# New instruction orders on five queues of an adaLN block with six local-attention layers, and one row transfer started before a wait

## The reference, cut to what matters

```python
h = layernorm(x) * (1 + ca) + sa;  x = x + ga * attention(h)      # 8 batches of 512 rows, 128 wide
h = layernorm(x) * (1 + cb) + sb                                  # goes through six layers of:
    h = attn_layer(shift_tokens(h), Wqkv[i], q_scale[i], k_scale[i], Wo[i]) + h
    h = ffn_layer(shift_tokens(h), ln_g[i], ln_b[i], W1[i], b1[i], W2[i], b2[i]) + h
x = x + gb * h
...
def attn_layer(x, Wqkv, qs, ksc, Wo):      # 16 heads of 64, windows of 32 rows
    q, k, v = split(x @ Wqkv)              # 128 -> 3 * 1024
    q = l2norm(q) * qs;  k = l2norm(k) * ksc
    q, k = rotate(q), rotate(k)            # cos part + rotated-half sin part
    p = softmax(8 * q @ k.T, masked)       # each window sees itself and the window before
    return (p @ v) @ Wo                    # 1024 -> 128
def ffn_layer(x, g, b, W1, b1, W2, b2):
    a, gate = split(layernorm(x) * g + b) @ W1 + b1)   # 128 -> 2 * 341
    return a * gelu(gate) @ W2 + b2
```

## Time and profile before

| | |
|---|---|
| time, median of 3 runs | 3615.62 us (3609.76 to 3617.31) |
| profiled execution: its own time / its span | 3607.98 us / 3606.2 us |
| PE busy | 3238.4 us (90% of the span) |
| DVE busy | 3119.3 us (86%) |
| POOL busy | 2468.9 us (68%) |
| ACT busy | 2391.9 us (66%) |
| granted PE clock, mean | 0.98 of full |
| DMA engines busy | 16 to 19% in the layers |

### The profile page before, as it was taken

How to read it: one execution, slowest core, us unless ns; L and a number is a source line. 1 busy time by engine, 2 the same in 40 slices (tenths; PEclk the granted TensorE clock), 3 DMA queues, 4 the chain that set the end, 5 groups by cost and what they waited for, 6 DMA issues and landing times.

```text
span 3606.2 us, 108351 instructions
## 1 busy us (share of the span) xinstructions
PE 3238.4 (90%) x46108; PEld 2099.0 (58%) x46108; DVE 3119.3 (86%) x2914; ACT 2391.9 (66%) x3945; POOL 2468.9 (68%) x1265
## 2 busy tenths in 40 slices
PE   5658999999999999999989999999999999999986
PEld 3325566666656666656656655666665666665663
DVE  6759989989989989989988998998998998998992
ACT  4645666666666766666666766666666666666664
POOL 4456776777777777767776777777776777776771
PEclk9879999999999999999999999999999999999997
DMA  2001111122111112111121111111211121111111
GB/s 76 1 1 36 39 37 40 37 55 53 38 37 39 41 48 55 40 39 37 36 54 49 42 39 38 40 49 48 48 37 37 38 53 49 44 39 40 37 38 40
DMA packets 150433, 148.32 MB, mean 41 GB/s; under 512 B 39228, under 2 KB 95424, under 8 KB 149952
## 3 DMA queue, kind: packets, MB, share of 16 engines
q1 hardware_dynamic: 149952, 141.39, 15.9%
HBM read 19.62 MB, written 2.10 MB: 6 GB/s over the span
## 4 chain that ended last, share of the span: by engine, by line
PE 48%; DVE 17%; issue 11%; SPq 9%; ACT 4%; DMA 3%; POOL 1%; ACTq 0%; DVEq 0%; POOLq 0%
PE bank L574 15%; PE mid L624 8%; PE bank L673 5%; PE mid L583 5%; PE bank L644 5%; SPq L345 4%; PE mid L611 4%; DMA PT<-PTd 3%; DVE PTd L1384 3%; DVE rot L1411 3%; PE bank L681 3%; DVE rot L1405 3%; PE mid L631 2%; SPq L352 2%; SPq L348 2%
## 5 line engine op out<-in xcount | busy, mean ns | idle before, releaser
L1155 POOL TENSOR_TENSOR swp<-raw,TS 128x1024 f32<-128x1024 f32 x384 | 899.8, 2368 | 823.7 <-DVE raw L1397 823.7
L574 PE MATMUL bank<-wqkv,xs 128*128 128x512 f32 x2304 | 1172.3, 614 | 82.0 <-ACT V L917 63.6
L1145 POOL TENSOR_TENSOR rr<-ssm,nhalf 128x32 f32<-128x32 f32 x192 | 1051.8, 5478 | 16.0
L903 ACT ACTIVATE raw<-bank 128x512 f32<-128x512 f32 x768 | 454.0, 598 | 341.0 <-PE bank L574 273.2
L574 PEld LDWEIGHTS bank<-wqkv,xs 128*128 128x128 f32 x2304 | 380.8, 190 | 366.1 <-issue 206.4
L1391 DVE TENSOR_REDUCE ss<-sq 128x16 f32<-128x1024 f32 x384 | 466.1, 1214 | 47.6 <-ACT sq L911 46.8
L583 PEld LDWEIGHTS mid<-ident,rot 128*128 128x128 f32 x3072 | 354.0, 141 | 225.9 <-issue 163.8
L1411 DVE TENSOR_TENSOR rot<-rot,swp 128x2048 f32<-128x2048 f32 x192 | 440.1, 2292 | 21.1 <-DVE rot L1405 1.4
L1397 DVE TENSOR_TENSOR raw<-raw,rr 128x2048 f32<-128x2048 f32 x192 | 438.0, 2281 | 14.4 <-POOL rr L1145 14.4
L624 PEld LDWEIGHTS mid<-PT,V 128*64 128x64 f32 x6144 | 338.4, 138 | 190.5 <-issue 139.3
L624 PE MATMUL mid<-PT,V 128*64 128x128 f32 x6144 | 382.4, 277 | 69.2 <-DMA PT<-PTd 61.8
(11 more groups left out here) (134 smaller groups left out, 4251.7 us busy)
## 6 DMA issues: line engine op xcount, KB each, us to landing
PT<-PTd SPq DMA_DIRECT2D x1344, 64.0 KB
xs<-F SPq DMA_DIRECT2D x192, 64.0 KB, 1.9
wqkv<-d_wqkv SPq DMA_DIRECT2D x36, 256.0 KB, 3.2
VT<-V SPq DMA_DIRECT2D x144, 64.0 KB
BT<-PTd SPq DMA_DIRECT2D x288, 32.0 KB
fwo<-d_fwo SPq DMA_DIRECT2D x6, 512.0 KB, 5.0
d_out<-X SPq DMA_DIRECT2D x8, 256.0 KB, 2.3
w<-d_w SPq DMA_DIRECT2D x6, 341.0 KB
```

What stands on the lines that cost most here:

```text
L574: nc.tensor.matmul(bank[bk][:, :], xs[:, j, :], wqkv[:, c, :], start=True, stop=True)\
L903: nc.scalar.activation(raw[:, j % 2, c * 512:(c + 1) * 512], bank[RAW_BANK[c]][:, :], ACT.Copy)\
L1145: pool.tensor_tensor(rr[:, :], ssm[:, :], nhalf[:, :], ALU.pow).then_inc(rr_ready, 1)
L1155: last = pool.tensor_tensor(dst[:, :, :, t, :], src[:, :, :, 1 - t, :], tab.unsqueeze(2).broadcast_to([P, 2, HEADS, 32]), ALU.mult)
```

## The change

Nothing is added to or taken from the computation; the number of instructions of each kind is the same. The change permutes the calls inside each `slot(c)`, moves some FFN stages into the next slot, and permutes a few DMAs. The PSUM bank of each projection follows from the new order.

```diff
-        LAST_QK = 1
+        LAST_QK = 2
         LAST_VO = 1
-        LAST_V = 4
-        RAW_BANK = (1, 0, 0, 1, 1, 0)
+        LAST_V = 5
+        RAW_BANK = (1, 0, 1, 0, 0, 1)
...
             def bands(n, j):
 
-                sp.wait_ge(pT_ready, n + 1)
                 wait(sp, pv_done, n)
                 if j > 0:
                     sp.wait_ge(v_out[1], n)
                     sp.dma_start(VT[P - 2 * W:P - W, :], V[P - W:P, 1 - j % 2, 512:1024]).then_inc(band_moved, 16)
+                sp.wait_ge(pT_ready, n + 1)
...
                 fetch(l, 4)
+                move(l, 0)
                 next_fwo(l)
-                move(l, 0)
```

More of the change, by code:

```diff
@@ L713, in slot @@
                     step(c, 4, out_proj)
+                    after_batch(c, (2, xn_ready), (3, yo_ready), (3, lin_out[2]), (3, ge_ready[2]), (3, ge_ready[1]), (3, ge_ready[0]), (3, lin_out[0]), (3, lin_out[1]), (3, nT_out))
+                    batch(c, 2, norm_back_ffn)
                 elif c % TPB == 1:
-                    after(c, (4, v_out[1]), (1, raw_out[2]), (1, raw_out[1]))
+                    after(c, (4, v_out[0]), (1, raw_out[3]), (1, raw_out[1]))
                     step(c, 0, proj, 1, True, 0)
+                    after_batch(c, (2, nT_out), (2, xn_ready), (3, yo_ready), (3, lin_out[2]), (3, ge_ready[2]), (3, ge_ready[1]), (3, ge_ready[0]), (3, lin_out[0]), (3, lin_out[1]))
@@ L717, in slot @@
+                    batch(c, 2, ffn_in, 1, 0, True, 7)
+                    after(c, (4, v_out[1]), (1, raw_out[2]), (1, raw_out[0]))
+                    step(c, 0, proj, 0, False, 1)
+                    after_batch(c, (2, lin_out[1]), (2, nT_out), (2, xn_ready), (3, yo_ready), (3, lin_out[2]), (3, ge_ready[2]), (3, ge_ready[1]), (3, ge_ready[0]), (3, lin_out[0]))
+                    batch(c, 2, ffn_in, 0, 0, False, 7)
                     after(c, (4, prob_ready))
                     step(c, 3, scores)
-                    after(c, (4, v_out[0]), (1, raw_out[3]), (1, raw_out[0]))
@@ L720, in slot @@
[L720 to L724, removed]
@@ L733, in slot @@
-                    after_batch(c, (2, lin_out[1]), (2, nT_out), (2, xn_ready), (3, yo_ready), (3, lin_out[2]), (3, ge_ready[2]), (3, ge_ready[1]), (3, ge_ready[0]), (3, lin_out[0]))
-                    batch(c, 2, ffn_in, 0, 0, False, 7)
+                    after(c, (3, qkT_out[1]), (5, oT_out), (3, qkT_out[3]))
+                    step(c, 2, qk_back, 3, True)
+                    after(c, (3, qkT_out[2]), (5, oT_out), (3, qkT_out[0]))
+                    step(c, 2, qk_back, 0, False)
+                    after(c, (0, raw_out[1]), (4, v_out[0]), (1, raw_out[3]))
@@ L735, in slot @@
+                    step(c, 0, proj, 3, False, 0)
+                    after(c, (0, raw_out[0]), (4, v_out[1]), (1, raw_out[2]))
+                    step(c, 0, proj, 2, False, 1)
                     after(c, (2, qkT_out[0]), (3, qkT_out[2]), (5, oT_out))
@@ L1006, in slot @@
                     step(c, 0, to_raw, 0, False)
+                    batch(c, 2, attn_to_sbuf)
                     step(c, 0, squares, 0)
+                    step(c, 2, qk_to_sbuf, 3)
                     step(c, 2, qk_to_sbuf, 0)
[L1009 removed]
+                    step(c, 0, to_raw, 3, False)
+                    step(c, 3, exps)
                     step(c, 0, to_raw, 2, False)
[L1011 to L1012 removed]
+                    step(c, 0, squares, 1)
                     step(c, 4, o_to_sbuf)
[L1014 removed]
                     step(c, 3, to_v, 4)
[L1016 removed]
+                    batch(c, 2, ffn_normed)
+                    batch(c, 2, ffn_affine)
                     step(c, 3, to_v, 5)
                     step(c, 2, qk_to_sbuf, 1)
[L1019 to L1020 removed]
+                    step(c, 2, qk_to_sbuf, 2)
+                    batch(c, 2, lin_to_sbuf, 1)
                 elif c % TPB == 1:
@@ L1060, in slot @@
                     step(c, 0, to_raw, 0, False)
+                    batch(c, 2, ffn_to_sbuf)
                     step(c, 0, squares, 0)
+                    step(c, 2, qk_to_sbuf, 3)
                     step(c, 2, qk_to_sbuf, 0)
-                    step(c, 2, qk_to_sbuf, 3)
+                    step(c, 0, to_raw, 3, False)
+                    step(c, 3, exps)
                     step(c, 0, to_raw, 2, False)
-                    step(c, 3, exps)
-                    step(c, 0, to_raw, 3, False)
+                    step(c, 0, squares, 1)
                     step(c, 4, o_to_sbuf)
-                    step(c, 0, squares, 1)
                     step(c, 3, to_v, 4)
-                    step(c, 2, qk_to_sbuf, 2)
                     step(c, 3, to_v, 5)
                     step(c, 2, qk_to_sbuf, 1)
-                    batch(c, 1, attn_to_sbuf)
+                    step(c, 2, qk_to_sbuf, 2)
             act.wait_ge(zero_ready, 1)
```

166 lines of the change are left out of this document (75 added, 91 removed).

## The result

The changed kernel takes 3455.81 us, the median of 4 runs (3452.98 to 3457.16), beside 3613.09 us for the kernel before on the same chip (4 runs, 3609.76 to 3617.31): a ratio of 0.9563, 95% interval [0.9547, 0.958]. The forecast was 3472 in 3430 to 3550.

The account below looks back on a forecast made before the run. PE and DVE wait for each other, neither the bound alone. One round, 11.4 + 16.9 + 7.3 + 4.2 + DVE's 14.3 and 11.05, makes 65.15 us against 68.2; over 47 intervals that saves 143 us: 3472, range 3430 to 3550.

Parts of the forecast that it names:

- The wait for OT: PE's `qk_back 1` waits for ACT's `o_to_sbuf`: about 0.9, 0.5, 0.7 and 0 us in slots 0 to 3.
- the squares ahead of `o_to_sbuf`: ACT, all four slots: a new wait; PE's `qk_back 1` can't start until 3.65 us after the exp.
- The covers of 1.5 us for the other moves: `centred` with its statistics, `attn_to_sbuf`, `ffn_to_sbuf`, weight loads: covers of 1.5 us or more, so no cost.
- DVE's 2.2 us before `sums`: DVE, slot 2: ready 2.2 us before the exp once a period, 100 us of waiting in all.
- VT: VT transfer issued ahead of the wait: bands arrive 0.57 us earlier, worth 0 to 0.57 a period.
- The table load: ACT, before slot 2's exp: 1.29 us is all it takes; a drain of about 1380 ns would give 3537 us.
- The second: Rival, 8%: DVE and POOL block each other where `gated` and `x_between` run beside `rotated` or `normed`; 3491 or 3590 us.
- A stretched L1397: Sign that the forecast is wrong: DVE's `normed` taking longer than its 2.28 us.
- The first rival: Rival, 12%: the new waits, `oT` late in four slots, are larger: 1.5 us a period more, about 3542 us.
- the third: Rival, 6%: slower; five bank7 handovers lose their cover, 0.95 us each, 4.8 a period instead of 0.5: 3672 us.
- the fourth: Rival, 2%: DVE's 4 us before `maxes` turn into as much before `sums` of slot 2: 3616 us.
- The fifth: Rival, 2%: the table load costs another 1.28 us where the exp follows a busy queue: 3532 us.

Follow-up runs that it names:

- experiment 2: Kernel before, with only ACT's copies of V5 and of q moved ahead of the three gelus in slot 1: 3545.69 us, ratio 0.9819.
- 1: Kernel before, with only the VT transfer moved ahead of the wait for the turned probabilities: 3569.9 us, ratio 0.9893.
- 4: Changed kernel, with the VT transfer put back behind the wait for the turned probabilities: 3472.95 us, ratio 0.962.
- Experiment 10: Changed kernel, with `x_between` cut from 513 columns to 33: 3455.85 us, ratio 0.9556.
- experiment 6: Changed kernel, with `o_to_sbuf` ahead of the squares of k again in all four ACT slots: 3638.27 us, ratio 1.0062.
- experiment 9: First two `gated` products cut to 32 columns: changed kernel 3456.95 us; third linear part behind slot 2's exp 3438.5; that exp also further forward 3425.93.
- experiment 5: Changed kernel, with `normed` put back behind `maxes` and `less_max` in all four DVE slots: 3714.19 us, ratio 1.0289.
- experiment 7: Changed kernel, with the third linear part put back behind the exp of slot 2: 3440.24 us, ratio 0.9514.

## Why the prediction was right

The time lies in the stated range, and the path that the forecast named, PE through slots 0 and 1, the exp chain, then DVE, is the one that the rows of this round show. Several waits inside it were wrong, and part of the close match is luck; both are told below.

**The period.** The forecast's sum, piece by piece, against the rows above. PE's slot 0 ran from the end of `rotated` (1913.47 + 2.29) to 1927.18, 11.4 us, forecast 11.4. Slot 1 to 1944.28: 17.1, forecast 16.9. Slot 2 up to `ffn_in(2, 0)` at 1951.70: 7.4, forecast 7.3. From there to `sums` at 1955.80: 4.1, forecast 4.2. DVE from there to the end of `rotated` at 1981.06: 25.3, forecast 25.35. Together 65.3 in this round, 65.0 over 47 periods.

The match of slots 0 and 1 is partly luck. By the forecast's own prices PE's work there is 10.5 and 16.0; on top of it I had put 0.9 and 0.5 for OT, and in this round PE waited for OT in neither. In their place stand 0.55 for FX in slot 0, 0.25 for the bands in slot 1, which the sum didn't have, and small gaps where a projection and an `ffn_in` alternate: 1.08, 0.93, 1.06 and 1.17 us from start to start at 1927.18 to 1931.42, priced at 0.86.

That PE's waits for V and for the q copy would go is shown by experiment 2, and that the bands' move counts by 1 and 4.

**The time.** 3455.8 is 16 below the 3472 given. The two profiled executions (3607.98 and 3455.64 us) differ by 152.3 where I had 143: 47 periods of 3.2 us are 150, the other 2 lie outside the layers' rhythm. The other 7.4 are an offset: I added 7.6 for the median above the profiled execution, and the changed kernel's median stands only 0.2 above its own.

**What was inside the sum and wrong, with its size.** *The wait for OT*: I put 2.1 us a period, 1.4 of it in the sum, and 100 us in all; PE waited 22.1 us, 0.5 a period. In slot 0, where I had 0.9, there is none: PE came later, because it had waited for FX before. Experiment 10 shows the two trade. And I called the squares ahead of `o_to_sbuf` only a new loss. The new order can't do without it: undone, it costs 180 us (experiment 6). PE can wait there, DVE cannot.

*The covers of 1.5 us for the other moves*: for `x_between` this was wrong. Blocked by `normed` it takes 3.37 us, and PE's `centred` waits 0.55. I had computed the cover with 1.3 for the product.

*DVE's 2.2 us before `sums`*: 59.0 us are 1.26 a period. Most of the rest is the longer `normed` right before it; without the blocking the wait is 99.4 / 47 = 2.1 (experiment 9). *VT*: 0 to 0.57 a period; undone, it costs 21 us, 0.45 a period. *The table load*: the exp began 1.29 after it (1953.46, 1954.75), as in the kernel before, with no drain of 1380 ns between; here the measurement differs from the Trainium skill's page (ScalarE: Activation LUTs) and decides.

**The rivals.** The second, DVE and POOL blocking each other, had its mechanism right and I argued against it with the wrong pair. A stretched L1397 was one of the signs of being wrong that I had named, and it came, at 3.37 us; the time didn't follow, because the stretch fell into the wait before `sums`, as that rival had it for slot 1. The power on POOL starts before `cos_part` in the stretch that I showed. Over the whole run before, the view is this:

```profile
L1145 POOL TENSOR_TENSOR rr<-ssm,nhalf x192: 5455/5457/7477, 233.4 to 3495.7; 128x32 f32<-128x32 f32 x192
```

The maximum of 7477 ns lay outside the window that I had taken: there are two such cases of 192, at 248.30 and 265.19 us. In experiment 5 it comes about once a period. One of them: the power is issued 0.09 us behind `cos_part` (2020.48, 2.25 long) and takes 2.02 longer than its 5.46, so it waited for `cos_part` to end.

```profile
2020.57 7.48 POOL L1145 TENSOR_TENSOR rr<-ssm,nhalf 128x32 f32<-128x32 f32 x1
```

The rival's price, 0.4 us a period beyond the covers, did not appear in the time of the changed kernel (experiments 9 and 10). The first rival (larger waits for OT), the third (lost covers of bank7) and the fourth (as much waiting before `sums` as before `maxes`) did not come. PE waited 0.5 us a period for OT. Its waits at the five handovers of bank7 were 1.9, 1.7, 0.8 and, for the gelus, 3.4 us in all. DVE's waits for scores and exp together were 68.5 us, after 252.9 before. The fifth (the load costing more) is answered above.

## What to carry to other kernels

When two engines are both near 90% and wait for each other, follow one round of the period through the queues with durations read start to start; here that gave the time to half a percent although single waits in it were wrong, because PE's waits replace each other (experiment 10). Then ask of each reordering which engine it makes wait: a new wait on the engine with slack can be worth having. And ask it of each move inside a change that wins, since one of them can be a loss (experiment 7). Last, look at the maximum of an instruction's duration over the whole run, with what the other engine was doing, before calling two engines free of each other.

## What the runs showed of the hardware

- A DVE tensor_tensor with two SBUF inputs and a POOL tensor_tensor on SBUF exclude each other in whole instructions, in both directions: `normed` 2.28 us became 3.37, the `gated` products' 1.27 became 2.16 and 3.31, `x_between`'s 1.1 to 1.3 became 3.37, and POOL's power, issued behind `cos_part`, 5.46 became 7.48.
- If the power starts first, `cos_part` keeps its 2.25: 2247 to 2252 ns over 164 tiles.
- POOL's busy time rose by 237 us through this, with the same instructions; most of it is waiting.
- One DMA issue of 0.57 us ahead of a band was worth 39 us in the old order and 21 in the new.
